# A fused transformer layer on one core: where a dequantisation scale runs, and when the last stage fetches its weights

## The reference, cut to what matters

```python
x = L0_attn_x                                   # 2048 tokens x 1024
x = x + layernorm(attention(layernorm(x)))      # 32 heads, causal
Wg, Wu, Wd = (dequantize(q, scale, zero) for ...)   # w = (nibble - zero) * scale, groups of 64
y = layernorm(x)
h = silu(y @ Wg.T) * (y @ Wu.T)                 # 2048 x 2752
return x + layernorm(h @ Wd.T)                  # 2048 x 1024
```

## Time and profile before

| | |
|---|---|
| median of 3 runs | 2721.6 us (2720.56 to 2721.88) |
| the profiled execution, its own time | 2721.11 us |
| its span, first to last instruction | 2719.3 us |
| PE / DVE / ACT / POOL busy | 96% / 68% / 37% / 43% of the span |
| mean granted clock of PE | 0.985 |
| gate stage, about | 1446 to 2265 us of the span |
| last stage, about | 2271 to 2719 us |

### The profile page before, as it was taken

The page is one execution under the profiler, slowest core; times in us unless marked ns, Lnnn a source line. Parts: engine busy times, 40 slices in busy tenths (PEclk is TensorE's granted clock), DMA queues, the critical chain, the costliest instruction groups (busy, mean ns, idle before and its releaser), DMA issues. The chain is left out here.

```text
span 2719.3 us, 42215 instructions
## 1 busy us (share of the span) xinstructions
PE 2604.5 (96%) x16888; PEld 1100.7 (40%) x16888; DVE 1855.4 (68%) x2329; ACT 997.5 (37%) x1755; POOL 1168.8 (43%) x641
## 2 busy tenths in 40 slices
PE   6999899999999999999997989999999999999998
PEld 3445533333333333323443434444444444444443
DVE  6331778777777877834668787777777763957755
ACT  3111266666666666672112223222223221210100
POOL 0000177777777777781223334555555550001001
PEclk9999999999999999999998999999999999999999
DMA  4223101011010110002233332333333327222331
GB/s 174 82 77 93 36 17 31 17 31 46 17 31 17 30 44 19 1 1 101 93 114 93 105 110 66 116 105 116 117 116 105 112 84 262 79 91 83 107 102 47
DMA packets 181131, 210.09 MB, mean 77 GB/s; under 512 B 18388, under 2 KB 139476, under 8 KB 180948
## 3 DMA queue, kind: packets, MB, share of 16 engines
q1 hardware_dynamic: 176176, 198.11, 22.7%
q10 hardware_dynamic: 4772, 9.44, 0.9%
HBM read 146.28 MB, written 61.08 MB: 76 GB/s over the span
## 5 line engine op out<-in xcount | busy, mean ns | idle before, releaser
L792 POOL TENSOR_TENSOR c_prob<-c_prob 128x1024 f32<-128x1024 f32 (+1 forms) x285 | 600.3, 2125 | 516.6 <-ACT c_prob L655 514.2
L674 DVE TENSOR_REDUCE c_maxes<-c_s 128x2 f32<-128x1024 f32 (+3 forms) x640 | 645.9, 1058 | 198.0 <-PE c_s L504 198.0
L655 ACT ACTIVATE c_prob<-c_s 128x512 f32<-128x512 f32 (+1 forms) x1152 | 597.9, 571 | 300.5 <-PE c_s L526 185.1
L526 PE MATMUL c_s<-c_q,c_k 97*128 97x512 f16 (+3 forms) x1280 | 367.3, 353 | 10.1 <-ACT c_prob L655 1.7
L1357 PE MATMUL e_ps<-x_hi,c_hi 128*128 128x512 f16 x832 | 316.9, 381 | 13.4 <-DVE c_hi L1432 10.5
L1358 PE MATMUL e_ps<-x_lo,c_hi 128*128 128x512 f16 x832 | 316.6, 381 | 0.0
L1359 PE MATMUL e_ps<-x_hi,c_hi 128*128 128x512 f16 x832 | 316.6, 381 | 0.0
L541 PE MATMUL c_ctx<-c_prob,v_sb 128*32 128x512 f32 (+3 forms) x2560 | 294.1, 541 | 0.2 <-ACT c_c L639 0.2
L1744 POOL TENSOR_TENSOR c_lo<-c_lo 128x1024 f32<-128x1024 f32 (+2 forms) x66 | 158.3, 2399 | 251.5 <-DVE c_lo L1416 251.5
L526 PEld LDWEIGHTS c_s<-c_q,c_k 97*128 97x128 f16 x1280 | 111.3, 97 | 346.4 <-ACT c_prob L655 298.3
L1771 POOL TENSOR_TENSOR e_hl<-e_h,e_hh 128x512 f16<-128x512 f32 (+1 forms) x88 | 141.0, 1610 | 190.3 <-ACT e_hh L1659 189.6
(11 more groups left out here) (246 smaller groups left out, 4409.9 us busy)
## 6 DMA issues: line engine op xcount, KB each, us to landing
h_hi<-e_hh SPq DMA_DIRECT2D x84, 128.0 KB, 1.9
h_lo<-e_hl SPq DMA_DIRECT2D x84, 128.0 KB, 1.7
b_x<-L_attn_x SPq DMA_DIRECT2D x16, 512.0 KB, 6.2
c_q<-qk_hi SPq DMA_DIRECT2D x64, 128.0 KB, 3.1
d_x<-L_attn_x SPq DMA_DIRECT2D x16, 512.0 KB, 4.7
x_dram<-d_x SPq DMA_DIRECT2D x16, 512.0 KB, 2.6
f_x<-x_dram SPq DMA_DIRECT2D x8, 1024.0 KB, 6.1
out<-f_z SPq DMA_DIRECT2D x16, 512.0 KB, 2.8
```

The costliest lines, as they stand in the source:

```text
L526: last = nc.tensor.matmul(S2[:, h % 2, at:at + w], K[:, g % 2, k * P:(k + 1) * P], Q[:, g % 2, b, h, q:q + w], start=True, stop=not diag)
L655: nc.scalar.activation(prob(g, s, 0, w)[:, h, :], S2[:, h % 2, 0:w], ACT.Exp, scale=exp_scale).then_inc(exp_done, 1)
L674: last = nc.vector.tensor_reduce(MAXES[:, g % 2, t // TPB, heads, t % TPB, u], S1[:, heads, at:at + w], AX.X, ALU.max)
L792: return nc.gpsimd.tensor_tensor(one, one, two, ALU.add)
```

## The change

Three things are changed, and a bookkeeping semaphore of the normalisation is dropped in the last stage.

1. For tasks 1 to 18 of the gate stage (`SCALED_HERE`, all that are prepared beside the plain units) DVE multiplies by the scales itself, right after subtracting the zeros. POOL scales only the later ones.
2. Of the last stage's weights, chunks 4, 5 and 6 are fetched behind the first four, by SP in the last unit of the gate stage, into the places in `c_hi` and `c_lo` that are no longer used. ACT's first part is then chunk 7 alone. Chunks 20 and 21 become a part of their own (`END`), the last that ACT issues, and PE waits for it only at chunk 20.
3. Round 1 (the second) takes chunks in the order 0 to 7, 20, 21, 8 to 19, and the rows of chunks 20 and 21 for round 2 are loaded as soon as round 1 is through with them, second after the part of chunk 4. ACT's and SP's waits follow the new order (`has_used`).

```diff
+    SCALED_HERE = range(1, 1 + max(k for u, ks in beside.items() if u[0] < PLAIN for k in ks))
...
-                    ready_by = 1 + max(downs.index((m, 1)) for m in range(FIRST // 2))
+                    ready_by = 1 + max(downs.index((m, 1)) for m in range(4))
...
+                    sp.wait_ge(cut_lo, cut_no[PAIRS - 1, "W2"])
+                    sp.wait_ge(down_lo, len(downs))
+                    for other, w in zip(first.others, (wd_hi, wd_lo)):
+                        sp.dma_start(other[:, 0:first.MORE, :], w[FIRST * P:(FIRST + first.MORE) * P, :]
+                                     .rearrange("(c p) d -> p c d", p=P)).then_inc(first.loaded, 16)
...
-                nc.vector.tensor_tensor(W[0:n, i, 0:planes, :], NIBBLES[0:n, 0:planes, :],
+                w = W[0:n, i, 0:planes, :]
+                nc.vector.tensor_tensor(w, NIBBLES[0:n, 0:planes, :],
                                         ZEROS[0:n, slot, :].unsqueeze(1).broadcast_to([n, planes, BANK]),
                                         ALU.subtract).then_inc(shifted, 1)
+                if k in SCALED_HERE:
+                    dve.wait_ge(shifted, k + 1)
+                    dve.wait_ge(scaled, k)
+                    nc.vector.tensor_tensor(w, w, SCALES[0:n, slot, :].unsqueeze(1).broadcast_to([n, planes, BANK]),
+                                            ALU.mult).then_inc(scaled, 1)
...
-            for k in range(1, AT_START):
-                scale(k)
             for u in units:
                 q, p = u
                 for k in beside.get(u, []):
-                    if k != ahead:
+                    if k not in SCALED_HERE:
                         scale(k)
...
-    parts = [(FIRST, 8), (8, 12), (12, 16), (16, FULL)]
+    parts = [(FIRST, 8), (8, 12), (12, 16), (16, PAIRED.stop), (PAIRED.stop, FULL + 1)]
+    END = len(parts) - 1
+    order = [[*range(FULL + 1)], [*range(8), *range(*parts[END]), *range(8, PAIRED.stop)]]
...
+        def has_used(r, c):
+
+            return (used, used_no[r, c]) if (r, c) in used_no else (product, product_no[r, "1"])
...
-                for i, (start, end) in enumerate(parts):
-                    if r:
-                        if end == FULL:
-                            sp.wait_ge(product, product_no[r - 1, "1"])
-                        else:
-                            sp.wait_ge(used, NJ * (r - 1) + (end - FIRST) // 2)
-                    load_chunks(r, start, end, part_loaded[i])
-                    if end == FULL:
+                for i in (0, END, 1, 2, 3) if r == PLAIN else range(len(parts)):
+                    start, end = parts[i]
+                    if i < END:
+                        if r:
+                            sp.wait_ge(*has_used(r - 1, end - 1))
+                        load_chunks(r, start, end, part_loaded[i])
+                    else:
+                        if r:
+                            sp.wait_ge(*has_used(r - 1, FULL))
+                        load_chunks(r, FULL - 1, FULL, part_loaded[i])
                         load_rest(r, part_loaded[i])
...
-                pe.wait_ge(first.loaded, 16 * 6)
-                for c in range(FULL + 1):
-                    for i, (start, end) in enumerate(parts):
+                pe.wait_ge(first.loaded, 16 * 8)
+                for c in order[r]:
+                    for i, (start, _) in enumerate(parts):
                         if c == start:
-                            pe.wait_ge(w_loaded[i], 16 * (6 if end == FULL else 2))
-                            pe.wait_ge(*part_rows(i, end, r))
+                            pe.wait_ge(*part_rows(i, r))
+                        if c == max(start, FIRST + first.MORE):
+                            pe.wait_ge(*part_weights(i))
...
                 if i == 4:
-                    act.wait_ge(used, NJ + j + 1)
+                    act.wait_ge(*has_used(PLAIN - 1, FIRST + 2 * j + 1))
```

More of the change, by code:

```diff
@@ L83, in on_vector @@
         dve.wait_ge(self.stats_done, 2 * r + 2)
-        dve.sem_inc(self.stats_seen, 1)
+        if self.stats_seen is not None:
+            dve.sem_inc(self.stats_seen, 1)
         for s in range(2):
@@ L1312, in _ @@
                     sp.wait_ge(product, product_no[units[-2] + ("P5",)])
-                    ready_by = 1 + max(downs.index((m, 1)) for m in range(FIRST // 2))
+                    assert PAIRS % 2 == 0 and FIRST + first.MORE <= 8
+                    ready_by = 1 + max(downs.index((m, 1)) for m in range(4))
                     sp.wait_ge(down_hi_stored, 16 * ready_by)
@@ L1854, with __init__ @@
 class First:
-    def __init__(self, tiles, loaded):
+    MORE = 3
+    def __init__(self, tiles, contexts, loaded):
         self.tiles, self.loaded = tiles, loaded
+        self.others = [c[:].rearrange("p k t -> p (k t)").rearrange("p (c d) -> p c d", d=2 * BANK) for c in contexts]
     def weights(self, i):
@@ L1899, in project_down @@
     product_no, join_no = numbered(products), numbered(joins)
+    used_no = {key: n + 1 for n, key in enumerate((r, c) for r in range(PLAIN) for c in order[r][:-1]
+                                                 if c == FULL or c in range(FIRST + 1, PAIRED.stop, 2))}
     banks = {"P1": 0, "D11": 1, "P2": 1, "D21": 2, "P4": 2, "D22": 3, "D12": 4, "P3": 4, "P6": 5, "P7": 6, "P5": 7}
@@ L1924, in project_down @@
         sb = lambda n, s, d=F32: ctx.enter_context(nc.sbuf_tensor("f_" + n, s, d))
-        wd = [c[:].rearrange("p k t -> p (k t)").rearrange("p (c d) -> p c d", d=D) for c in (c_hi, c_lo)]
+        wd = first.others
         wd_end = [sb(n, [P, FULL + 1 - PAIRED.stop, D], F16) for n in ("wd_end_hi", "wd_end_lo")]
@@ L2075, in plain @@
                             o = PS[:, 4 * (r % 2) + 2 * s + n, :]
+                            final = c == order[r][-1]
                             if c == FULL:
-                                last = rest(o, H[0][:, FULL, at], columns(c, n), True)
+                                last = rest(o, H[0][:, FULL, at], columns(c, n), final)
                             else:
                                 a = [first.rows(i, r)[:, c, at] if c < FIRST else H[i][:, c, at] for i in range(2)]
-                                last = chunk(o, a, columns(c, n), c == 0, False)
-                        if c == FULL:
+                                last = chunk(o, a, columns(c, n), c == 0, final)
+                        if final:
                             last.then_inc(product, 1)
-                    if PAIRED.start <= c < PAIRED.stop and (c - FIRST) % 2:
+                    if (r, c) in used_no:
                         last.then_inc(used, 1)
@@ L2116, in strassen @@
                 if r == PLAIN:
-                    for i, (_, end) in enumerate(parts[:-1]):
-                        pe.wait_ge(*part_rows(i, end, r))
+                    for i in range(END):
+                        pe.wait_ge(*part_rows(i, r))
                 else:
@@ L2141, in make_t1_to_t3 @@
                 t1, t2, t3 = (t_sum(i, j) for i in (1, 2, 3))
+                if j == 0:
+                    dve.wait_ge(first.loaded, 16 * 8)
                 for i, (start, end) in enumerate(parts):
-                    if start == FIRST + 2 * j:
-                        dve.wait_ge(w_loaded[i], 16 * (6 if end == FULL else 2))
+                    if max(start, FIRST + first.MORE - 1) == FIRST + 2 * j:
+                        dve.wait_ge(*part_weights(i))
                 if j:
@@ L2253, in _ @@
                 if r == PLAIN:
-                    for i, (_, end) in enumerate(parts):
-                        dve.wait_ge(*part_rows(i, end, r))
+                    for i in range(END):
+                        dve.wait_ge(*part_rows(i, r))
                     dve.wait_ge(cut_lo, t_no(4, NJ - 1))
@@ L2286, in _ @@
                 for buf, over, src in zip(wd, wd_end, (w_hi, w_lo)):
[L2287 to L2291 removed]
+                    if i < END:
+                        start = max(start, FIRST + first.MORE)
+                        act.dma_start(buf[:, start - FIRST:end - FIRST, :], src[start * P:end * P, :]
                                       .rearrange("(c p) d -> p c d", p=P)).then_inc(w_loaded[i], 16)
[L2293 removed]
+                    else:
+                        act.dma_start(over[:, 0, :], src[(FULL - 1) * P:FULL * P, :]).then_inc(w_loaded[i], 16)
+                        act.dma_start(over[:, 1, :], src[FULL * P:, :].unsqueeze(0).broadcast_to([2, REST, D])
                                       ).then_inc(w_loaded[i], 16)
```

29 lines of the change are left out of this document (13 added, 16 removed).

## The result

| | before | after |
|---|---|---|
| median | 2721.74 us (2720.56 to 2722.34, 4 runs) | 2697.94 us (2694.62 to 2698.28, 4 runs) |
| the profiled execution | 2721.11 us | 2698.28 us |
| its span | 2719.3 us | 2696.5 us |
| gate stage, PE's first matmul to PE's first of the last stage | 824.85 us | 817.99 us |
| last stage, PE's first matmul to the end of the span | 448.75 us | 432.10 us |

The kernel is faster: ratio 0.991, 95% interval 0.9893 to 0.9928. Forecast were 2700 us and a range of 2691 to 2709. The profiled spans differ by 22.8 us: 6.86 from the gate stage and 16.65 from the last stage, less 0.71, by which this execution entered the gate stage later (1446.41 against 1445.70), before anything of the change has run.

A forecast was written before the change was run, and what follows sets the result against it. PE was taken to bound the kernel, busy nearly throughout, so only its waits and clock falls could be gained: 8.9 + 7.5 + 5.0 = 21.4 us off 2721.11, 2699.7, forecast as a 2700 us median, range 2691 to 2709.

The forecast's parts named there:

- Last stage, 16.4 us predicted: Last stage: removing PE's waits at chunk 16 and at round 2's start gains 8.9 and 7.5 us.
- The two waits: Last stage: PE's 5.94 us at chunk 16 of round 0 and 4.56 us at the start of round 2 both go.
- The clock falls: Last stage: after each of its two waits, 14 matmuls at half clock cost about 3.0 us.
- the first term: Chunk 16 of round 0: the end part, due only at chunk 20, lands with 8 us to spare; gain 8.9 us.
- the slow tail: Last stage's weight load: a few DMA engines finish alone at 115 GB/s; the split only moves this.
- The extra fetch: End of the gate stage: two 768 KB transfers on SP, 2 us allowed each, cost nothing.
- Round 2: Last stage: normalisation ends 7.7 us after round 1; P6 does not wait for its sums, with 2.7 us to spare.
- Rival B: Last stage: one wait survives in another form, likeliest P6 of round 2 or a late end part; 2708 us, chance 0.13.
- Gate stage, 5.0 us predicted: Gate stage: DVE scaling instead of POOL shortens PE's waits for W2; gain 5.0 us, bounds 2 and 8.
- DVE's chain: Gate stage, from about 1510 to W2 of pair 4: DVE's sequence of operations gets 7.9 us shorter.
- the chain from there to P7: Gate stage, W2 of pair 4 to P7 of unit (5, 0): DVE's added scales make it 0.65 us longer.
- The price of the exclusion: Gate stage: each POOL scale followed by a DVE operation from SBUF holds DVE 2.15 us; the added multiplication costs 1.27.

The follow-up runs named there:

- e2: The changed kernel without the gate stage's DVE scaling and without the new chunk order of round 1: 2711.49 us.
- e3: The kernel before with only round 1's new order and early rows for chunks 20 and 21, whose weights are issued last but awaited at chunk 16: 2712.8 us.
- e5: The changed kernel, but PE waits at chunk 16 for the weights of chunks 20 and 21 too: 2699.47 us.
- e4: The kernel before with the chunk 21 transfer issued as two transfers of 64 rows instead of one with leading dimension 2: 2711.33 us.
- e6: The changed kernel with nothing fetched ahead beyond chunk 3, the split of chunks 20 and 21 kept: 2699.22 us.
- e7: The changed kernel with each added DVE multiplication by the scales done twice: 2712.76 us.
- e0_after_again: The changed kernel itself, unchanged, run again beside the kernel with DVE's sums on the same chip: 2697.58 us.

## Why the prediction was right, step by step

**Last stage, 16.4 us predicted, 16.65 measured.** The two waits were 5.94 and 4.56 us, and both are gone. The clock falls behind them cost 2.8 and 2.9 us by the starts of the matmuls in the timeline; I took 3.0 each. That makes 16.2. I left out that a matmul is recorded with 0.38 us while the next one starts 0.216 us after it: the idle time is counted from the end of the record, so each wait hides 0.16 us more. With these the sum is 16.5 of 16.65, and my total came closer than its terms, since 0.3 us too much for the clock stood against 0.3 us left out. The parts alone showed that the two terms are separate (e2, e3).

**The reason given for the first term was only half of it.** I held that the end part lands at 2316, that is 45.5 us into the stage, and is needed 8 us later. e5 has it at 44.5. But I treated the slow tail as given ("not shortened by the split but only moved"), and the fetch ahead as part of the cure. Shortening the tail is enough by itself: e4 removes the wait without any of the change. The fetch ahead isn't needed once the part is split (e6).

**The extra fetch** cost nothing, as said, and even less than allowed. SP's queue after, the fetch and then the stage's last stores:

```profile
2252.06 0.63 SPq L1336 DMA_DIRECT2D c_hi<-wd_hi  x1
2252.73 0.60 SPq L1336 DMA_DIRECT2D c_lo<-wd_lo  x1
...
2262.34 0.32 SPq L1351 DMA_DIRECT2D h_hi<-e_hh  x1
2263.64 0.32 SPq L1353 DMA_DIRECT2D h_lo<-e_hl  x1
```

They took 0.6 us an issue instead of the 2 I allowed. That the queue had been full at the 3.36 us of the earlier trace rows was my reading, and no run tests it. The wait between the stages is 5.16 us as before.

**Round 2.** The normalisation of round 1 was to end 7.7 us after the round, and P6 to have 2.7 us to spare. The timeline of DVE after:

```profile
2383.53 2.60 DVE L99 TENSOR_SCALAR f_z<-f_ps,f_norm_mv,f_norm_rstd 128x1024 f32<-128x1024 f32 x2
...
2405.28 0.69 DVE L2221 TENSOR_TENSOR f_s_lo<-f_sums,f_s_hi 128x512 f16<-128x512 f32 x1
```

Round 2 starts at 2378.53, the normalisation ends at 2386.13 (7.6 us later; the dropped increment saves about 0.1 us of it, 0.71 us from the last statistics to the aggregation where before had 0.82), the sums are ready at 2405.97 and P6 starts at 2408.74: 2.8 us to spare. Rival B missed by these 2.8 us.

**Gate stage, 5.0 us predicted, 6.9 measured.** The mechanism and its signs held: the added operation takes 1.22 to 1.23 us, DVE's operations beside it are back at 0.68, no operation is stretched but those that meet other work of POOL, its trails above all. The waits came as foreseen, 1.91 us for 2.6 and 3.72 for 2.4 or 4.5, and the clock with them: kept after the first, lost after the second, at 2.5 us for the 2.2 taken. The term that was off is DVE's chain. It was to gain 7.9 us up to W2 of pair 4 and gained 8.8 (PE starts at 1600.00 instead of 1608.11, in a stage that began 0.71 later). And the chain from there to P7 was to lose 0.65 us and lost nothing:

```profile
1598.63 1.22 DVE L1450 SCALAR_TENSOR_TENSOR c_hi<-c_lo,c_hi 128x1024 f16<-128x1024 f32 x1
...
1643.96 1.21 DVE L1450 SCALAR_TENSOR_TENSOR c_hi<-c_lo,c_hi 128x1024 f16<-128x1024 f32 x1
```

W2 of pair 4 to W2 of pair 5 is 45.3 us; before it was 45.5. I had charged three added multiplications to this stretch in full and counted too little of what they set free. Together the chain was 1.75 us better than I made it (P7 gained 9.0 us, not 7.2). The clock took 0.3 us more than I gave it, and the fourth wait of 0.2, which I left where it was, went too. These are most of the 1.9 us by which the stage, and of the 2 us by which the forecast, was off.

**The price of the exclusion.** I took 2.15 us of standing for each scale with an SBUF operation of DVE behind it. By line it comes to 19.7 us over 12 tasks, two of them of half the rows: 1.6 us a task, for 1.34 us added. That is a thin margin. Of the 8.9 us by which DVE's chain is shorter, 3.6 are this margin, 3.3 are DVE's shorter wait for the down chunks, and 1.7 the operations that make W with their waits for ACT. The rule of the Trainium skill ("SBUF — State Buffer", "Who interferes with whom") also held in the direction that speaks against the edit: where a trail of POOL runs, the new operation takes 2.06 us. Three of the twelve meet one here, two of full size and one of half the rows. One of them:

```profile
1565.69 2.15 POOL L1789 TENSOR_TENSOR e_hl<-e_h,e_hh 64x512 f16<-64x512 f32 x1 [0.86 <-ACT e_hh L1677]
...
1566.87 2.06 DVE L1435 TENSOR_TENSOR c_lo<-c_lo 128x1024 f32<-128x1024 f32 x1
```

## What to carry to other kernels

When an engine waits for a transfer while few of the DMA engines work, look at the shape of the last transfer before moving data earlier: here the last piece in two transfers instead of one removed the same wait as a re-cut of the whole load. Before an elementwise step goes to GpSimd to relieve a full VectorE, compare VectorE's durations with and without GpSimd running beside it; if the same line has two durations, the help may cost more than the work. And a wait is priced with the clock behind it, so cutting one from 3.7 to 1.4 us can be worth more than the difference.

## What the runs showed besides

- Waits of much the same length can cost the clock differently: after 5.94 us the next 6 us ran at 0.52, after 5.54 us (e3) at 0.77. By the starts of the matmuls the falls in these runs cost between 1.3 us (5.54 us in e3, 4.04 us in e7) and 2.9 us (4.56 us in before), and the longest wait, 8.73 us, cost 2.1.
- Executions of one kernel differ by some 4 us through what happens ahead of the gate stage. In `e0_after_again` the profiled execution (2694.57 us) enters it at 1442.14 instead of 1446.41, and both take 818 us from there. The expectation had put such runs down to a smaller loss at P7; but PE stands 3.70 us there and loses 2.7 us to the clock, no less than in after. The stretch from 120 to 300 us ran at a clock of 1.00 there, at 0.98 in the profile of after:

```profile
120.00:300.00 180.00, 172.15 (x1039) 94.02 (x1037) 66.36 (x92) 26.83 (x46) 0.00 (x0) 1.00 0.22 71
```

```profile
120.00:300.00 180.00, 172.58 (x1021) 93.87 (x1020) 64.97 (x89) 26.85 (x46) 0.00 (x0) 0.98 0.24 72
```

The first row is of that execution, the second of after's. A comparison by stage from PE's first matmul of the stage is finer than the medians.
